# Two short units of each attention head: fp32 probabilities times fp32 values, value products issued three units behind

## The reference, cut to what matters

```python
q, k, v = (proj(Wq), proj(Wk), proj(Wv))          # B=2, S=1024, 16 heads of 32
q = q * cos + rotate_half(q) * sin
k = k * cos + rotate_half(k) * sin
scores = jnp.einsum('bhqd,bhkd->bhqk', q, k) / math.sqrt(HD)
scores = jnp.where(causal, -jnp.inf, scores)
attn = jax.nn.softmax(scores, axis=-1)
out = jnp.einsum('bhqk,bhkd->bhqd', attn, v)
```

## Time and profile before

| | |
|---|---|
| median of 3 runs | 3494.87 us (3492.46 to 3495.08) |
| the profiled execution, its own time | 3502.3 us |
| span of its trace | 3500.5 us |
| PE, DVE, ACT, POOL busy over the span | 83%, 57%, 34%, 27% |
| granted TensorE clock, mean | 0.917 |
| front phase | about 0 to 197 us |
| attention of the first layer | about 197 to 757 us, first scores at 259 us |

### The profile page before, as it was taken

The page is one execution under the profiler, slowest core; times in us unless marked ns, Lnnn a source line. Parts: engine busy times, 40 slices in busy tenths (PEclk is TensorE's granted clock), DMA queues, the critical chain, the costliest instruction groups (busy, mean ns, idle before and its releaser), DMA issues. The chain is left out here.

```text
span 3500.5 us, 42242 instructions
## 1 busy us (share of the span) xinstructions
PE 2895.0 (83%) x14636; PEld 2302.5 (66%) x14636; DVE 2011.0 (57%) x3642; ACT 1202.6 (34%) x2343; POOL 950.9 (27%) x664
## 2 busy tenths in 40 slices
PE   7938888876999999347899999579999994488994
PEld 6825555554888888236688888467888883366773
DVE  5628778756233232435466666655666666667655
ACT  2206555542111111113344444224444442233331
POOL 1206666653111111203100000140000001267743
PEclk9958889987999999678899999899999997699997
DMA  4542222213000100672000000300000002111002
GB/s 163 196 150 70 81 96 82 76 50 114 19 19 19 36 0 1 189 278 100 26 32 31 21 31 21 131 35 25 32 21 31 21 27 102 67 37 37 0 1 96
DMA packets 111743, 224.36 MB, mean 64 GB/s; under 512 B 9376, under 2 KB 55456, under 8 KB 110848
## 3 DMA queue, kind: packets, MB, share of 16 engines
q1 hardware_dynamic: 111616, 222.72, 18.4%
HBM read 155.84 MB, written 66.58 MB: 64 GB/s over the span
## 5 line engine op out<-in xcount | busy, mean ns | idle before, releaser
L1041 POOL TENSOR_TENSOR l0a_probs_hl<-l0a_probs,l0a_probs_hl 128x896 fp32r<-128x896 f32 (+1 forms) x128 | 293.4, 2311 | 229.6 <-ACT l0a_probs L963 229.6
L1273 PE MATMUL l1a_obank<-l1a_pT_hl,l1k_v_hl 128*128 128x512 f32 (+3 forms) x1152 | 300.4, 370 | 7.2 <-DVE l1a_pT_hl L1346 7.1
L1346 DVE TENSOR_TENSOR l1a_pT_hl<-l1a_work,l1a_pT_hl 128x512 fp32r<-128x512 f32 (+3 forms) x384 | 212.9, 555 | 155.1 <-ACT l1a_pT_hl L1306 154.9
L1299 ACT ACTIVATE l1a_probs<-l1a_scores,l1a_row 128x128 f32<-128x128 f32 (+7 forms) x256 | 189.3, 741 | 317.9 <-DVE l1a_row L1336 317.9
L1253 PE MATMUL l1a_scores<-l1k_kT_hl,l1a_qa_hl 128*128 128x512 f32 (+3 forms) x1152 | 291.6, 361 | 1.5 <-ACT l1a_probs L1299 1.5
L1389 POOL TENSOR_TENSOR l1a_q_stage<-l1k_qpe,l1a_ones 128x512 fp32r<-128x512 f32 x32 | 33.3, 1040 | 875.4 <-PE l1a_work L1281 818.4
L962 ACT ACTIVATE l0a_probs_hl<-l0a_sbank 128x896 fp32r<-128x896 f32 (+1 forms) x192 | 156.2, 813 | 258.9 <-PE l0a_sbank L934 194.8
L1678 DVE TENSOR_TENSOR f0f_hid<-f0f_silu,f0f_ubank 128x512 f32<-128x512 f32 x64 | 44.1, 688 | 322.2 <-PE f0f_ubank L1613 322.2
L1306 ACT CAST l1a_pT_hl<-l1a_work 128x512 fp32r<-128x512 f32 (+3 forms) x384 | 183.6, 478 | 107.3 <-PE l1a_work L1264 106.1
L948 PE MATMUL l0a_obank<-l0a_probs_hl,l0a_v_stage 128*96 128x512 f32 (+3 forms) x768 | 195.6, 380 | 28.3 <-DVE l0a_probs_hl L1002 23.7
L1281 PE MATMUL l1a_work<-l1a_wov,l1a_oT_hl 128*128 128x512 f32 x768 | 214.2, 401 | 5.0 <-DVE l1a_oT_hl L1365 3.0
(11 more groups left out here) (254 smaller groups left out, 6324.6 us busy)
## 6 DMA issues: line engine op xcount, KB each, us to landing
qk_dram<-l0f_stage SPq DMA_DIRECT2D x8, 2048.0 KB, 9.5
l1a_wov<-wov_dram SPq DMA_DIRECT2D x32, 512.0 KB, 3.4
v_dram<-l0f_v_rows SPq DMA_DIRECT2D x16, 768.0 KB, 3.7
l0a_v_stage<-v_dram SPq DMA_DIRECT2D x8, 1536.0 KB, 9.2
l1a_wabs<-wabs_dram SPq DMA_DIRECT2D x32, 384.0 KB, 3.8
l0a_q_stack<-qk_dram SPq DMA_DIRECT2D x32, 256.0 KB
l0a_k_stack<-qk_dram SPq DMA_DIRECT2D x32, 256.0 KB
wov_dram<-w1a_wov SPq DMA_DIRECT2D x16, 512.0 KB, 3.3
```

What stands on the lines that cost most here:

```text
L1041: nc.gpsimd.tensor_tensor(probs_hl[:, r, 1, 0:wide], probs[:, r, 0:wide], f32(probs_hl[:, r, 0, 0:wide]), ALU.subtract).then_inc(low_done[ ...
L1273: last = pe.matmul(obank[:, c:SPAN], src["v_hl"][:, a, n, :], pT_hl[:, ring(n, s), b, c:SPAN], start=(n == 0 and i == 0), stop=(n == QT * ...
L1299: nc.scalar.activation(probs[s][:, first:first + wide, :].rearrange("p k c -> p (k c)"), scores[:, n % S_AHEAD, 0:wide * P], ACT.Exp, bias ...
L1346: nc.vector.tensor_tensor(pT_hl[:, r, 1, c:SPAN], work[:, slot, c:SPAN], f32(pT_hl[:, r, 0, c:SPAN]), ALU.subtract).then_inc(work_free[slo ...
```

## The change

1. The short units (`IN_FP32 = (1, 5)`) get no high and no low part: ACT makes `exp` of them once, in fp32, DVE's subtraction L1002 is gone, and PE multiplies the fp32 probabilities with fp32 values, one product for each of the two key tiles where there were two.
2. The fp32 values have to come from somewhere: the front writes for every second pair of tiles (8 of 16 tiles) a second array `v32_rows` (32 zeros, 32 ones, 32 values for each head), stores it (768 KB for each such tile) in `v32_dram`, and the attention loads half as much again for each group, behind the loads of `v_stage`.
3. Value products are issued LAG = 3 steps behind the exponential instead of 1, O four instead of 2; the ring has 6 slots instead of 4, and the steps of SP, DVE and POOL that hang on them move by two.

```diff
@@ front_layer0 @@
+    v32_rows = m.sb("v32_rows", [P, 2, NH, 3 * HD0])
...
                 sp.dma_start(v_dram[b, :, tt].rearrange("g p c -> p g c"),
                              f32(v_rows[:, t % 2].rearrange("p (g j) c -> p g (j c)", g=KT))).then_inc(v_stored[t % 2], 16)
+                if tt in KT_FP32:
+                    sp.wait_ge(v32_made, made_upto(t))
+                    sp.dma_start(v32_dram[b, :, KT_FP32.index(tt)].rearrange("g p c -> p g c"),
+                                 v32_rows[:, t % 2].rearrange("p (g j) c -> p g (j c)", g=KT)).then_inc(v32_stored[t % 2], 16)
...
                     act.wait_ge(full[2], t + 1)
+                    if t % TB in KT_FP32:
+                        wait(act, v32_stored[t % 2], 16 * ((made_upto(t) - 1) // 2))
+                        nc.scalar.copy(v32_rows[:, t % 2, :, 2 * HD0:3 * HD0], in_heads(t)).then_inc(v32_made, 1)
                     wait(act, v_stored[t % 2], 16 * (t // 2))
...
             for slot in range(2):
                 nc.vector.tensor_copy(v_rows[:, slot, :, HD0:2 * HD0], ones[:, :, None].to_broadcast([P, NH, HD0])
                                       ).then_inc(ones_set, 1)
+                nc.vector.memset(v32_rows[:, slot, :, 0:HD0], 0.0).then_inc(ones_set, 1)
+                nc.vector.memset(v32_rows[:, slot, :, HD0:2 * HD0], 1.0).then_inc(ones_set, 1)
@@ constants and steps @@
-RING0 = 4
+LAG = 3
+RING0 = LAG + 3
-LOWS_BY_DVE = (1, 5)
+IN_FP32 = (1, 5)
+KT_FP32 = [kt for kt in range(TB) if kt % QT >= 2]
...
-        if 0 <= i - 1 < HEADS * U:
-            yield "P", i, i - 1
-        if 0 <= i - 2 < HEADS * U and (i - 2) % U in (1, U - 1):
-            yield "O", i, 2 * ((i - 2) // U) + ((i - 2) % U == U - 1)
+        p, o = i - LAG, i - LAG - 1
+        if 0 <= p < HEADS * U:
+            yield "P", i, p
+        if 0 <= o < HEADS * U and o % U in (1, U - 1):
+            yield "O", i, 2 * (o // U) + (o % U == U - 1)
@@ attention_layer0, SP @@
                 sp.dma_start(f32(v_stage[:, slot].rearrange("p t j c -> p t (j c)")),
                              v_dram[b, g].rearrange("t p c -> p t c")).then_inc(v_loaded[slot], 16)
+                sp.dma_start(v32_stage[:, slot].rearrange("p t j c -> p t (j c)"),
+                             v32_dram[b, g].rearrange("t p c -> p t c")).then_inc(v_loaded[slot], 16)
...
-                if k == 3 and h >= 1 and (h - 1) % GROUP_HEADS == GROUP_HEADS - 1 and (h - 1) // GROUP_HEADS + 2 < GROUPS:
+                if k == LAG + 2 and h >= 1 and (h - 1) % GROUP_HEADS == GROUP_HEADS - 1 and (h - 1) // GROUP_HEADS + 2 < GROUPS:
                     load_values((h - 1) // GROUP_HEADS + 2)
-                if k == 3 and 0 <= h - 1 < HEADS:
+                if k == LAG + 2 and 0 <= h - 1 < HEADS:
                     store_sums(h - 1)
-                group, late = divmod(i - (U * (GROUP_HEADS - 1) + 9), U * GROUP_HEADS)
+                group, late = divmod(i - (U * (GROUP_HEADS - 1) + 8 + LAG), U * GROUP_HEADS)
@@ attention_layer0, PE @@
-                    mine, count = lows_upto(n)
-                    pe.wait_ge(low_done[mine], count)
+                    if u in IN_FP32:
+                        pe.wait_ge(exp_done, n + 1)
+                    else:
+                        pe.wait_ge(low_done, lows_upto(n))
...
+                        if u in IN_FP32:
+                            steps = [(v32_stage[:, group % 2, KT_FP32.index(kt), j, :], probs[:, r, span])]
+                        else:
+                            steps = [(v_stage[:, group % 2, kt, j, :], probs_hl[:, r, part, span]) for part in range(2)]
@@ attention_layer0, ACT and DVE @@
-                    nc.scalar.activation(probs_hl[:, r, 0, 0:wide], sbank[:, n % 2, 0:wide], ACT.Exp)
+                    if n % U not in IN_FP32:
+                        nc.scalar.activation(probs_hl[:, r, 0, 0:wide], sbank[:, n % 2, 0:wide], ACT.Exp)
...
-                elif kind == "L" and n % U in LOWS_BY_DVE:
-                    _, _, wide = pieces(n % U)
-                    r = n % RING0
-                    dve.wait_ge(exp_done, n + 1)
-                    nc.vector.tensor_tensor(probs_hl[:, r, 1, 0:wide], probs[:, r, 0:wide],
-                                            f32(probs_hl[:, r, 0, 0:wide]), ALU.subtract).then_inc(low_done[True], 1)
```

More of the change, by code:

```diff
@@ L535, in front_layer0 @@
     v_stored = [m.sem(f"v_stored{i}") for i in range(2)]
+    v32_made = m.sem("v32_made")
+    v32_stored = [m.sem(f"v32_stored{i}") for i in range(2)]
+    made_upto = lambda t: sum(i % TB in KT_FP32 for i in range(t + 1))
     use = front_uses()
@@ L573, in _ @@
                 if t == 0:
-                    sp.wait_ge(ones_set, 3)
+                    sp.wait_ge(ones_set, 7)
                 sp.wait_ge(read[2], t + 1)
@@ L582, in _ @@
                 sp.wait_ge(v_stored[i], 16 * NT // 2)
+                sp.wait_ge(v32_stored[i], 16 * made_upto(NT - 1) // 2)
                 sp.wait_ge(qk_stored[i], 16 * NT // 4)
@@ L724 @@
 U = len(UNITS)
-FIRST, LAST = -2 * U, HEADS * U + 2
+FIRST, LAST = -2 * U, HEADS * U + LAG + 1
 MAX_PARTS = [(t, c) for t in range(TB) for c in range(0, (t + 1) * P, SPAN)]
-LOWS_BY_DVE = (1, 5)
+IN_FP32 = (1, 5)
+KT_FP32 = [kt for kt in range(TB) if kt % QT >= 2]
 def pieces(u):
@@ L743, in lows_upto @@
     h, u = divmod(unit, U)
-    mine = u in LOWS_BY_DVE
-    per = len(LOWS_BY_DVE) if mine else U - len(LOWS_BY_DVE)
-    return mine, h * per + sum((v in LOWS_BY_DVE) == mine for v in range(u + 1))
+    return h * (U - len(IN_FP32)) + sum(v not in IN_FP32 for v in range(u + 1))
 def steps_layer0():
@@ L775, in uses_layer0, with attention_layer0 @@
     return out
-def attention_layer0(nc, m, ident, ident_bf, mask, qk_dram, v_dram, sums_dram, inverse_dram, out, next_load):
+def attention_layer0(nc, m, ident, ident_bf, mask, qk_dram, v_dram, v32_dram, sums_dram, inverse_dram, out, next_load):
     mbank = m.ps("mbank", [P, 2, SPAN])
@@ L892, in _ @@
                         load_inverse(group)
-            for group in range((HEADS * U + 23 - (U * (GROUP_HEADS - 1) + 9) - 10) // (U * GROUP_HEADS) + 1, GROUPS):
+            for group in range((HEADS * U + 23 - (U * (GROUP_HEADS - 1) + 8 + LAG) - 10) // (U * GROUP_HEADS) + 1, GROUPS):
                 load_sums(group)
@@ L940, in _ @@
                     if u == 0 and j == 0:
-                        pe.wait_ge(v_loaded[group % 2], 16 * (group // 2 + 1))
+                        pe.wait_ge(v_loaded[group % 2], 32 * (group // 2 + 1))
                     if parts[0][0] == 0:
                         wait(pe, o_done, 2 * (h - 1) + s + 1)
-                    mine, count = lows_upto(n)
-                    pe.wait_ge(low_done[mine], count)
+                    if u in IN_FP32:
+                        pe.wait_ge(exp_done, n + 1)
+                    else:
+                        pe.wait_ge(low_done, lows_upto(n))
                     for kt, c, at, _ in parts:
[L947 to L950, removed]
-                                             stop=(kt == QT * (s + 1) - 1 and part == 1))
+                        span = slice(at, at + SPAN - c)
+                        if u in IN_FP32:
+                            steps = [(v32_stage[:, group % 2, KT_FP32.index(kt), j, :], probs[:, r, span])]
+                        else:
+                            steps = [(v_stage[:, group % 2, kt, j, :], probs_hl[:, r, part, span]) for part in range(2)]
+                        for part, (values, weights) in enumerate(steps):
+                            last = pe.matmul(obank[0:3 * HD0, s, c:SPAN], values, weights, start=(kt == 0 and part == 0),
+                                             stop=(kt == QT * (s + 1) - 1 and part == len(steps) - 1))
                     last.then_inc(values_done, 1)
@@ L1036, in _ @@
             for kind, i, n in steps_layer0():
-                if kind == "L" and n % U not in LOWS_BY_DVE:
+                if kind == "L" and n % U not in IN_FP32:
                     _, _, wide = pieces(n % U)
@@ L1041, in _ @@
                     nc.gpsimd.tensor_tensor(probs_hl[:, r, 1, 0:wide], probs[:, r, 0:wide],
-                                            f32(probs_hl[:, r, 0, 0:wide]), ALU.subtract).then_inc(low_done[False], 1)
-                group, late = divmod(i - (U * (GROUP_HEADS - 1) + 9), U * GROUP_HEADS)
+                                            f32(probs_hl[:, r, 0, 0:wide]), ALU.subtract).then_inc(low_done, 1)
+                group, late = divmod(i - (U * (GROUP_HEADS - 1) + 8 + LAG), U * GROUP_HEADS)
                 if kind == "P" and late == 14 and 0 <= group < GROUPS - 1:
@@ L2052, in two_layers @@
                 front_layer0(nc, m, ident, x0, [view(f"L0_attn_W{n}") for n in "qkv"],
-                             tuple([a[f"{n}_{w}0"] for w in "qk"] for n in ("cos", "sin")), qk_dram, v_dram)
+                             tuple([a[f"{n}_{w}0"] for w in "qk"] for n in ("cos", "sin")), qk_dram, v_dram, v32_dram)
             with phase("l0") as keep:
```

8 lines of the change are left out of this document (5 added, 3 removed).

## The result

| | before | changed |
|---|---|---|
| median of 4 runs each, us | 3494.97 (3492.46 to 3497.95) | 3541.03 (3532.88 to 3547.49) |
| ratio to before, with its 95% interval | 1 | 1.013 (1.0105 to 1.0155) |
| profiled execution and its span, us | 3502.3, 3500.5 | 3544.96, 3543.2 |
| first step after the attention on PE (L132), us | 757.1 | 799.2 |

The change costs 46 us, and the interval of the ratio leaves no room for noise. Attention ends 42.1 us later and the span is 42.7 us longer, so the loss lies ahead of L132. The forecast was 3507, at most 3532.

What follows compares the result with a forecast made beforehand. The prediction took the loop between PE and DVE to bound each head, then SP's queue. Its terms, 8.4 - 5.2 + 3.8 + 1.7 + 3.6, gave +12.3 us: 3507 us from the median; forecast's own range 3492 to 3525, overall 3474 to 3532.

Steps and rivals of the forecast that it cites:

- Value loads: Attention, one head of four: both value loads right behind the stack on two engines; a new PE wait of 5.5 us.
- What it drags along: Attention, SP's queue after those loads: later stacks and rows of N come late; +1.4 us in each of six groups, +8.4.
- The high end: Attention, dearest case: 14.1 us a head, values 4.4 and 2.2, 2 us of low clock; +37, 3532 us.
- Short units on DVE: Attention, each head: L1002 goes, and with it PE's waits of 0.84 and 1.10 us; -1.94 us.
- On PE: Attention, short units: fp32 products 0.77 us at most against 0.60; between +0.17 and +0.25 each, +0.4 a head.
- Output instructions behind the maxima: Attention, DVE: L1010 and L1013 stand between the joining and N, so N ends later; 0 to +1.2 us, taken +0.7.
- the heads without loads: Attention, heads 0 to 3 and two near the end: 13.2 us a head instead of 14.07; -5.2 us.
- Start and front: Stage start: fp32 value loads ahead of N's first rows, +3.8 us; front: memsets +1.7, stores of fp32 tiles +3.6.
- rival "faster": Attention: the rows of N aren't held up and PE never waits for SP; 3470 us, chance 0.24.
- The fit quoted there: Skill's rule for one DMA: some 2 us plus bytes at 436 GB/s, so a stack through in about 4 us.
- Low clock after each wait: Attention rival: PE runs at 1.2 GHz after its waits; 3 us a group, 3525 us and more, chance 0.12.
- Doesn't do what it says: Attention rival: the loop is held by PE alone; 14.07 us a head, 3518 us, no chance of its own.

Runs made afterwards that it cites:

- the split: Each stack load of 2 x 32 rows issued as two loads of 32 rows: changed kernel 3424.5 us (ratio 0.9808), kernel before 3447.8 us (0.9868).

## Why the prediction was wrong

- **Direction and mechanism** held: the short loop got shorter, and the value loads behind the stack made SP's queue the bound, with long waits in six heads and smaller ones two heads later. The size was off by nearly a factor of four: +12 forecast, +46 measured.
- **The step that failed is "Value loads"**, the service of the two engines. It put stack and values one behind the other at the pace each had alone: 12.1 + 3.7 + 1.9 = 17.7 us. They took 21.9, since the stack on two engines and the values on the others slow each other while both run (231 GB/s instead of 312). The largest part is the term that seemed safe, the stack itself: "stack to 13.4", 12.1 us, took 15.8; the values behind it went on for 6.1 where 5.6 was forecast. The 12.1 came from a stack with no value load near it, the 3.7 from a load that had been *ahead* of a stack, which is just the order that the change gave up; in that order a stack took 12.1 us before and 12.2 with the value loads moved ahead. So PE went on at 24.1, not 19.9.
- **What it drags along** followed from it: the next late rows came at 55.4 instead of 50.2. Four heads took 66.0 to 69.4 us between stack issues, 67.6 in the mean, for 62.7 forecast: 4.9 x 6 = 29 of the 30 us that the span missed. Of the 4.9, the waits for N's rows make 2.7 (8.8 + 1.6 = 10.4 us a group for 5.5 + 2.2; 62.9 in all for 30 to 50), the heads 1.0 (4 x 13.45 for 4 x 13.2), and 1.2 is the rest: 3.4 us are left beside waits and heads, where the forecast had 2.2, 0.7 of them low clock. The low clock can explain that: behind the wait that ends at 565 us PE is busy all of 5 us at 1.2 GHz, up to 2.5 us lost by an estimate from these rows (us, busy time of PE, PEld, DVE, ACT, POOL, clock, DMA share, GB/s):

```profile
565.00:570.00 5.00, 5.00 (x17) 3.44 (x17) 1.16 (x2) 2.18 (x3) 1.67 (x1) 0.50 0.28 73
570.00:575.00 5.00, 3.54 (x18) 2.22 (x17) 4.26 (x10) 1.97 (x3) 1.01 (x2) 0.91 0.15 53
```

 The high end was 65.9 us for four heads, still too low: it widened the values, the period and the low clock, but left the stack at 12.1.
- **Short units on DVE** held: both waits are gone. **On PE** a unit of true fp32 takes 0.84 us at full clock for the 0.60 of the earlier trace rows, +0.24, at the upper end of the step. That is over the 0.8 us that the prediction named as a sign of being wrong on PE; with +0.5 a head for +0.4 the term was a little small.

```profile
296.68 0.84 PE L973 MATMUL l0a_obank<-l0a_probs,l0a_v_stage 128*96 128x256 f32 x4
```

- **Output instructions behind the maxima**: forecast 0 to 1.2, taken 0.7; the trace has a wait of 1.2 us in nearly each head (35.0 us in 29). A head took 13.45, not 13.2, and the heads without loads gave about -4 for -5.2.
- **Start and front**: the first scores came 11.0 us later for 9.1 forecast, the stage began 6.6 us later for 5.3 (203.7, before 197.1).
- **The rival "faster"** failed as argued: N's rows were held up. What it stood on, a stack on all engines, is what the split made true, and then the change does gain. The fit quoted there is one that the Trainium skill gives for DMAs issued by GpSimd, and these are SP's, so the 12.0 us don't speak against the page. **"Low clock after each wait"** was named at 3 us a group, near the 2.5 estimated above, and it added to the forecast instead of taking its place. **"Doesn't do what it says"** is out: 13.45, not 14.07.

## What to carry to other kernels

Before adding bytes or moving a load, ask which DMA engines each transfer occupies, and put small rows that someone waits for ahead of large ones. A load on few engines and one on all of them don't add up from their times alone: here each slowed the other while both ran, and a price taken from one order didn't hold in the other. And when products are deferred, look at what their consumers now stand in front of on their own engine.

## What the runs showed that was not expected

- One DMA of 2 x 32 rows of 4 KB against two of 32 rows: two more issues a stack, 0.5 us of SP, gave 44 us in the kernel before. 33 of them are the start, where the third head begins at 246.4 us for 279.3; 9 come from the heads behind it (L132 at 715.3 us for 757.1), in which PE had waited only 4.2 us for N's rows.
- A DMA issue can itself wait: L848 stood 10.65 us on SP behind a stack and a value load, 0.57 us with the loads ahead. Everything behind it in the program of SP was issued that much later.
- The granted clock of the stage was higher with fewer waits of PE: 0.89 with 98 us of waits for DMA and N's slot, 0.99 with 36 us. How much of the gain of the split is that, no run tells apart.
